# Three moves in a two-layer gated cross-attention kernel: context moments taken early, wider layer-norm chains, and expert products in split fp32r

## Chip, cores and metric

One core of one Trainium2 chip. The metric is the device time of one execution in microseconds (us), launch to end. The core has five engines with a queue each: TensorE (PE, with its weight loads shown apart as PEld), VectorE (DVE), ScalarE (ACT), GpSimd (POOL) and SyncE (SP, which here only issues transfers). They run side by side and meet at semaphores; each engine takes its own instructions strictly in the order in which the program lists them.

## What is computed

Two layers over x (4 batches of 256 tokens, 128 features) and a context (4 batches of 512 tokens, 128 features):

```python
x = x + tanh(g_xattn[0]) * L0_xattn(layernorm(x), ctx)       # 16 heads of 8, q and k normalised per head
x = x + tanh(g_ffn[0])   * L0_ffn(layernorm(x))              # shared gated FFN, top-2 of 8 LoRA experts
x = x + tanh(g_xattn[1]) * L1_xattn(ctx, layernorm(x))       # 16 heads of 64
x = x + tanh(g_ffn[1])   * L1_ffn(layernorm(x))              # top-1 of 8 full experts

def L1_xattn(c, latents):            # queries from latents, keys and values from both
    c, lat = layer_norm(c, ln_m_g, ln_m_b), layer_norm(latents, ln_l_g, ln_l_b)
    kv_in = concat(c, lat)
    ...
def L1_ffn(x):
    idx = argmax(softmax(x @ gate_w + gate_b, axis=1), axis=-1)
    for e in range(8):
        h = gelu(x @ W1[e] + b1[e])                          # 128 -> 512
        out += where(idx == e, h @ W2[e] + b2[e], 0)         # 512 -> 128
```

A layer norm is (t - mean) * rsqrt(var + 1e-5) over the 128 features. The context's mean and variance depend on the input `ctx` alone, the tokens' on the running x.

## The kernel before

Everything stays in on-chip memory; a token tile is 128 tokens, so a batch has TQ = 2 token tiles and TC = 4 context tiles. The order of work is written out by hand for every engine, one function per step of an engine, and steps of different engines meet at one semaphore per kind of step.

**First attention** (about 47 to 190 us). `AQ` = 16 turns of four heads each. In turn q PE makes score maxima of turn q+2 (`row_max0`, eight products into two banks in turn), scores of turn q (`scores0`), values of turn q-1; ACT the exponentials; POOL four multiplies per turn that mask the queries (`masked0`, L513); DVE eight maxima (L1047) and one `divide0` (L1054, L1058). A product of `row_max0` may write its bank only when DVE has read the product two before it.

**First FFN** (190 to 300 us). One pass per batch: DVE runs `hidden0`, `route0`, `norm_b`, `down0`, `lora0`, `residual_b`. After batch 0 DVE also takes the moments and the reciprocal root of context batch 0 and normalises it (`context_stats(0)`, `context_scale(0, 0)`, `context_scale(0, 1)`, `context_norm(0)`), after batch 1 the same for the tokens of batch 0.

**Second attention** (300 to 711 us). `G1` = 32 pairs of heads; g = 8 b + p is pair p of batch b. Per pair DVE has three row maxima (`row_max1`, L1291 and L1294, and the small L1300 `max_cols`), two low halves of the projections of pair g+3 (`proj_low`, L1282 `kql`), and a division (`divide1`, L1307 `RECIPROCAL` and L1308). Two slots per pair, `first_slot(g)` (before the third maximum) and `second_slot(g)` (after it), hold the preparation of the next batch: for b < 3 the moments (p = 0), the reciprocal root by halves (p = 1, 2) and the normalising (p = 3), of context in the first slot and of tokens in the second. For b = 3 they hold the norms of token batches 0 and 1 for the last stage, and its first routing. Each reciprocal root is a chain of dependent instructions on 128x4 or 128x2 values: L1216 or L1232 first, then L1201, L1202 and three (first half) or six (second half) of L1205, L1206, L1207. PE issues the products of all this in a fixed order; in pair p = 1 of batches 1 to 3 it also makes the output projection of the batch before (`outputs1`, 32 fp32 instructions into bank 7, which the half 1 of `project(g+3)` used just before: it waits until `proj_low(g+3, 1)` has read it). POOL sums the exponentials (L540, L543, L548).

**Second FFN** (711 us to the end). Per batch i: PE `hidden1(i, 0..3)`, each 8 fp32 products of 128x128 weights and 256 masked token columns (`xm`) and one bias product; ACT the gelu and a rounded copy `hid1_h`; POOL the low part `hid1_l` in two halves (L556); PE `down1(i, 0)`, `down1(i, 1)` in split fp32r. A split product is three fp32r products, high by high, high by low, low by high. In between PE, ACT and DVE route batch i+1: `turned_in1`, `head1`, `route1`, softmax, `probs1`, `masks1`, `wide_masks1`, `masked` (DVE writes `xm` in two halves, L1394), `bias1`. An fp32 product appears in the trace as two matmul instructions, an fp32r product as one.

## Time and profile before

| | us |
|---|---|
| median of 3 runs (850.34 to 851.39) | 851.11 |
| the profiled execution | 852.44 |
| its span, first to last instruction | 850.4 |

The profiled execution is thus 1.33 us over the median, and 2.04 us of it lie around the span.

```profile
PE 748.1 (88%) x5558; PEld 550.1 (65%) x5558; DVE 587.3 (69%) x1169; ACT 357.6 (42%) x528; POOL 287.9 (34%) x207
PEclk9789999997999999999998999899999999999999
PE 64%; DVE 24%; issue 7%; ACT 3%; DMA 1%; POOL 0%; SPq 0%; POOLq 0%; DVEq 0%; ACTq 0%
```

The first line is busy time, share of the span and instructions of each engine. The second cuts the span into 40 slices and gives the TensorE clock granted in each, in tenths of full speed, 2.4 GHz. The third is the chain of work that ended last, by engine. Matmul ends are modelled, and matmuls overlap: the rate of a run of matmuls is read from the distance of their starts, not from their durations.

### The profile page before, as it was taken

How to read it: one execution, taken by the hardware profiler on the slowest of the kernel's cores; microseconds unless marked ns; L12 is line 12 of the kernel's file. 1: busy time of each engine (PE TensorE's matmuls, PEld its weight loads, DVE VectorE, ACT ScalarE, POOL GpSimd, SP SyncE). 2: the span in 40 equal slices, each digit the busy share in tenths (PEclk: the TensorE clock that was granted, in tenths of full speed). 3: DMA queues.
4: the chain of work that ended last, by engine and by line, in shares of the span. 5: the costliest groups of instructions: out<-in, count | busy, mean ns of one | idle time of the engine just before them, and what ended most of it. 6: DMA issues, size and time to landing. Idle time of an engine off the chain costs nothing.

```text
span 850.4 us, 14161 instructions
## 1 busy us (share of the span) xinstructions
PE 748.1 (88%) x5558; PEld 550.1 (65%) x5558; DVE 587.3 (69%) x1169; ACT 357.6 (42%) x528; POOL 287.9 (34%) x207
## 2 busy tenths in 40 slices
PE   6779999977888978899979998889989878989896
PEld 5656666646777755667656675656756556867784
DVE  4767676727887777886878769787788784446243
ACT  2567676653342454355524553245534443130200
POOL 4364443300111023455533455245543462010100
PEclk9789999997999999999998999899999999999999
DMA  9000000013000030000000000000000000000000
GB/s 173 6 1 2 1 3 1 2 67 132 1 1 1 0 99 1 2 1 2 1 1 2 1 2 1 1 2 1 2 1 2 1 1 1 1 7 2 6 7 6
DMA packets 25553, 11.55 MB, mean 14 GB/s; under 512 B 11832, under 2 KB 24200, under 8 KB 25360
## 3 DMA queue, kind: packets, MB, share of 16 engines
q1 hardware_dynamic: 24480, 10.59, 4.9%
q8 instruction: 44, 0.72, 0.3%
q10 hardware_dynamic: 1008, 0.07, 0.1%
q14 instruction: 21, 0.17, 0.1%
HBM read 10.06 MB, written 0.52 MB: 12 GB/s over the span
## 4 chain that ended last, share of the span: by engine, by line
PE 64%; DVE 24%; issue 7%; ACT 3%; DMA 1%; POOL 0%; SPq 0%; POOLq 0%; DVEq 0%; ACTq 0%
PE ps L1536 61%; DVE pmax L1294 2%; DVE kql L1282 2%; DVE o L1307 2%; PE ps L1547 2%; DVE rt_t L1206 1%; DVE pmax L1291 1%; DVE max_cols L1300 1%; ACT v L562 1%; ACT kqh L562 1%; DVE ysum L1413 1%; DVE cn L948 1%; DVE rs_t L924 1%; DVE rt_t L1205 1%; DVE xnC L1239 1%
## 5 line engine op out<-in xcount | busy, mean ns | idle before, releaser
L803 ACT ACTIVATE p<-ps 128x1024 f32<-128x1024 f32 x96 | 96.4, 1025 | 147.1 <-PE ps L1536 144.7
L1536 PE MATMUL ps<-p,v 128*64 128x256 f32 (+1 forms) x1280 | 131.4, 388 | 5.1 <-DVE o L1308 2.3
L540 POOL TENSOR_TENSOR acc<-p 128x1024 f32<-128x1024 f32 x32 | 76.7, 2397 | 168.7 <-ACT p L803 168.7
L1536 PE MATMUL ps<-kqh 64*128 64x256 f32 (+1 forms) x640 | 106.6, 371 | 12.5 <-DVE pmax L1291 4.7
L1047 DVE TENSOR_REDUCE mx<-ps 128x1 bf16<-128x512 f32 x128 | 82.5, 687 | 36.3 <-PE ps L1536 36.0
L1291 DVE TENSOR_REDUCE pmax<-ps 128x2 f32<-128x1024 f32 x64 | 78.2, 1222 | 39.2 <-PE ps L1536 38.3
L543 POOL TENSOR_TENSOR acc<-acc,p 128x1024 f32<-128x1024 f32 x32 | 76.2, 2380 | 70.7 <-ACT p L803 70.7
L1536 PEld LDWEIGHTS ps<-p,v 128*64 128x64 f32 (+1 forms) x1280 | 63.7, 126 | 54.9 <-issue 19.3
L1536 PEld LDWEIGHTS ps<-kqh 64*128 64x128 f32 x640 | 59.0, 195 | 38.3 <-issue 28.7
L513 POOL TENSOR_SCALAR q<-qst,rmask 128x256 fp32r<-128x256 f32 x64 | 58.7, 936 | 59.0 <-ACT qst L562 59.0
L658 ACT ACTIVATE p<-ps 128x1024 f32<-128x1024 f32 x64 | 65.4, 1025 | 22.3 <-PE ps L1536 20.4
L1282 DVE TENSOR_TENSOR kql<-ps,kqh 128x512 fp32r<-128x512 f32 x64 | 44.1, 690 | 26.9 <-ACT kqh L562 26.4
L1536 PE MATMUL ps<-xm,w 128*128 128x256 f32 x256 | 58.7, 381 | 2.7 <-DVE xm L1394 2.7
L1307 DVE RECIPROCAL o<-ps 128x256 f32<-128x256 f32 x32 | 56.1, 1752 | 5.9 <-PE ps L1536 4.3
L1536 PE MATMUL ps<-max_row,onesb 64*128 64x256 bf16 x384 | 57.2, 284 | 0.0
L1536 PE MATMUL ps<-kqh,kql 64*128 64x256 f32 x384 | 56.9, 283 | 0.0
L1536 PE MATMUL ps<-kql,kqh 64*128 64x256 f32 x384 | 56.3, 279 | 0.0
L1536 PEld LDWEIGHTS ps<-xm,w 128*128 128x128 f32 x256 | 47.4, 190 | 10.7 <-DVE xm L1394 3.5
L556 POOL TENSOR_TENSOR hid_l<-hid,hid_h 128x512 fp32r<-128x512 f32 x8 | 10.1, 1264 | 115.2 <-ACT hid_h L562 115.2
L1536 PE MATMUL ps<-kst,q 128*128 128x512 f32 x128 | 47.2, 427 | 0.8 <-DVE mx L1047 0.5
L1536 PE MATMUL ps<-q,kst 128*128 128x256 f32 x256 | 46.7, 304 | 0.4 <-ACT p L658 0.4
L1294 DVE TENSOR_REDUCE pmax<-ps 128x4 f32<-128x1024 f32 x32 | 39.1, 1222 | 10.1 <-PE ps L1536 9.7
(268 smaller groups left out, 1526.2 us busy)
## 6 DMA issues: line engine op xcount, KB each, us to landing
w<-in_L_ffn_W_dram SPq DMA_DIRECT2D x1, 2048.0 KB, 12.6
wt<-in_L_ffn_W_dram SPq DMA_DIRECT2D x4, 512.0 KB, 6.1
ctx_all<-in_ctx_dram SPq DMA_DIRECT2D x4, 256.0 KB, 5.2
raw_kv<-in_L_xattn_Wkv_dram SPq DMA_DIRECT2D x1, 1024.0 KB, 5.1
raw<-in_L_ffn_B_dram SPq DMA_DIRECT2D x9, 64.0 KB
xr<-in_x_dram SPq DMA_DIRECT2D x4, 128.0 KB, 3.8
raw_q<-in_L_xattn_Wq_dram SPq DMA_DIRECT2D x1, 512.0 KB, 6.1
wout<-in_L_xattn_Wout_dram SPq DMA_DIRECT2D x1, 512.0 KB, 7.4
```

What stands on the lines that cost most here:

```text
L513: pool.tensor_scalar(q4[:, q % SLOTS, v, :], qst[:, q % 2, :], rmask[:, v:v + 1], None, ALU.mult).then_inc(g_q4.sem, 1)
L540: pool.tensor_tensor(acc1[:, :], p1[:, s, 0, :], p1[:, s, 1, :], ALU.add).then_inc(g_acc.sem, 1)
L543: pool.tensor_tensor(acc1[:, :], acc1[:, :], p1[:, s, 2, :], ALU.add).then_inc(g_acc.sem, 1)
L562: return act.activation(to, of, ACT.Copy)
L658: act.activation(p0[:, n % PR0, :], bank(2 * (n % 2), 2), ACT.Exp).then_inc(a_exp0.sem, 1)
L803: act.activation(p1[:, g % 2, u, :], bank(2 * (n % 2), 2), ACT.Exp, scale=SCALE1).then_inc(a_exp1.sem, 1)
L1047: dve.tensor_reduce(mx0[:, q % 2, n % 2, n // 2:n // 2 + 1], bank(4 + m % 2), AX, ALU.max).then_inc(d_max0.sem, 1)
L1282: dve.tensor_tensor(kql[:, g % KS, at], bank(X_BANK.get(("proj", g, half), 7)), kqh[:, g % KS, at], ALU.subtract).then_inc(d_kql.sem, 1)
L1291: dve.tensor_reduce(pmax[:, g % 2, 0, part, :], m.rearrange("p (j k) -> p j k", j=2), AX, ALU.max).then_inc(d_max1.sem, 1)
L1294: dve.tensor_reduce(pmax[:, g % 2, 1, :, :].rearrange("p t j -> p j t"), m.rearrange("p (j t k) -> p j t k", j=2, t=TQ), AX, ALU.max).then ...
L1307: then(dve.reciprocal(o1[:, g % OS, :], bank(6)[:, NQ:2 * NQ]))
L1536: return pe.matmul(o, lhsT, rhs, start=start, stop=stop)
```

## The change

1. **Context moments.** A new `spare_slot(q)` at the end of each turn of the first attention on DVE: q = 2 to 5 take the moments of context batch q-2, q = 6 and 7 the two halves of the reciprocal root of all 16 tiles at once. The calls in the first FFN and in the slots of the second attention go; only `context_norm` stays.
2. **Shared token chains.** The tokens of batches 1 to 3 have their moments taken in pair 0 and their reciprocal root in pair 1 of the second attention, together. The norms of batches 0 to 2 for the last stage have theirs in pairs 2 and 3 of batch 3 and are applied in pair 4 (0 and 1) and later (2). Several small steps of the last pairs move too.
3. **Expert input products** of batches 1 to 3 become split fp32r: ACT rounds `w1` to `w1_h` in four parts, DVE makes `w1_l`, ACT and DVE split the tokens, DVE writes masked high and low tokens instead of one `xm`. The steps of PE, ACT and DVE in the last stage are put in another order, and the second half of `hid1_l` goes from POOL to DVE.

Left out of the diff below: new buffers and semaphores, and functions that only get new index arguments.

```diff
+            def spare_slot(q):
+                if 2 <= q < 2 + B:
+                    context_stats(q - 2)
+                if q - 2 - B in (0, 1):
+                    context_scale(q - 2 - B)
...
                 if q >= 1:
                     divide0(q - 1)
+                spare_slot(q)
...
                 if i == 0:
-                    context_stats(0)
-                    context_scale(0, 0)
-                    context_scale(0, 1)
                     context_norm(0)
...
             def first_slot(g):
+                if b + 1 < B and p == 3:
+                    context_norm(b + 1)
+                if g == 0:
+                    dve.wait_ge(d_xB.sem, B)
+                    dve.wait_ge(d_xnC.sem, 1)
+                    tokens_stats(range(TQ, 2 * TQ), 0)
+                if g == 1:
+                    tokens_scale(rest, 0, True)
+                if b == B - 1:
+                    if p == 2:
+                        tokens_stats(range(0, 2 * TQ), 0)
                     if p == 3:
+                        tokens_scale(rest, 0, False)
                     if p == 4:
+                        tokens_norm(xnD[:, 0, :, :], x_of(0), 0).then_inc(d_xnD.sem, 1)
+                    if p == 6:
+                        masks1(0)
+            def second_slot(g):
+                if b + 1 < B and p == 3:
+                    latents_norm(b + 1)
+                if g == 0:
+                    tokens_stats(range(2 * TQ, B * TQ), TQ)
+                if g == 1:
+                    tokens_scale(rest, 1, True)
+                if b == B - 1:
+                    if p == 2:
+                        tokens_stats(range(2 * TQ, 3 * TQ), 2 * TQ)
+                    if p == 3:
+                        tokens_scale(rest, 1, False)
+                    if p == 4:
+                        tokens_norm(xnD[:, 1, :, :], x_of(1), TQ).then_inc(d_xnD.sem, 1)
                         step(dve.memset(probT[:, :], 0.0))
                     if p == 5:
                         route1(0)
...
                 second_slot(g)
                 if g + 3 < G1:
                     proj_low(g + 3, 1)
+                if g == G1 - 1:
+                    masked(0, 0)
                 if g >= 1:
                     divide1(g - 1)
                 if g == G1 - 3:
                     probs1(0)
+                    w2_low(0)
                 if g == G1 - 2:
+                    w2_low(1)
                     wide_masks1(0)
                 if g == G1 - 1:
-                    masked(0, 0)
-                    w2_low(FC - 1)
                     masked(0, 1)
+                    w2_low(2)
+                    w2_low(3)
             divide1(G1 - 1)
             for i in range(B):
                 if i + 1 < B:
                     route1(i + 1)
+                    tokens_low(i + 1)
                     probs1(i + 1)
+                if i == 0:
+                    for c in range(E // 2):
+                        w1_low(c)
+                if i + 1 < B:
                     masks1(i + 1)
                     wide_masks1(i + 1)
+                hidden_low(i)
                 if i == 0:
                     residual_c(B - 1)
+                if i + 2 < B:
+                    norm_d(i + 2)
+                if i + 1 < B:
+                    masked(i + 1, 0)
                 select1(i, 0, 0)
                 select1(i, 0, 1)
                 if i + 1 < B:
-                    masked(i + 1, 0)
+                    masked(i + 1, 1)
                 summed1(i, 0)
-                if i + 2 < B:
-                    norm_d(i + 2)
                 select1(i, 1, 0)
                 select1(i, 1, 1)
-                if i + 1 < B:
-                    masked(i + 1, 1)
                 summed1(i, 1)
                 residual_d(i)
...
             bias_out(0)
+            w1_high(0)
             for i in range(B):
                 if i + 1 < B:
                     routed(i + 1)
+                    act.wait_ge(a_xTD.sem, i + 2)
+                    copy(xT_h[:, (i + 1) % 2, :], xTD[:, (i + 1) % 2, :]).then_inc(a_xTh.sem, 1)
+                    if i == 0:
+                        for c in range(1, E // 2):
+                            w1_high(c)
+                    softmax(i + 1)
                 for n in range(2):
...
                 for e in range(E):
                     if c == 0 and e % 4 == 0:
                         pe.wait_ge(d_xm.sem, 2 * i + e // 4 + 1)
+                    if i == 0:
+                        mm(o, w1[:, e, c * P:(c + 1) * P], xm[:, e, :], e == 0, False)
+                        continue
+                    if i == 1 and c == 0 and e % 2 == 0:
+                        pe.wait_ge(d_w1L.sem, e // 2 + 1)
+                    mm(o, w1_h[:, e, at], xm_h[:, e, :], e == 0, False)
+                    mm(o, w1_h[:, e, at], xm_l[:, e, :], False, False)
+                    mm(o, w1_l[:, e, at], xm_h[:, e, :], False, False)
...
+                if g == G1:
+                    wide_masks1(0, 1)
+                    bias1(0)
                 if g >= 1:
                     values1(g - 1, (0, 1, 2, 3))
...
             for i in range(B):
                 ahead = i + 1 < B
+                if ahead:
+                    turned_in1(i + 1)
                 hidden1(i, 0)
                 if ahead:
-                    turned_in1(i + 1)
+                    head1(i + 1)
                 hidden1(i, 1)
                 if ahead:
-                    head1(i + 1)
+                    probs1(i + 1)
                 hidden1(i, 2)
-                if ahead:
-                    probs1(i + 1)
                 hidden1(i, 3)
                 if ahead:
                     masks1(i + 1)
                 if i == 0:
                     outputs1(B - 1)
-                down1(i, 0)
                 if ahead:
                     wide_masks1(i + 1, 0)
-                down1(i, 1)
+                down1(i, 0)
                 if ahead:
                     wide_masks1(i + 1, 1)
                     bias1(i + 1)
+                down1(i, 1)
```

## Rows read from the trace of the kernel before

**Rows 1.** Engine busy time by stretch: us, busy (instructions) of PE, PEld, DVE, ACT, POOL; PEclk, DMA
```profile
414.00:462.00 48.00, 41.17 (x337) 29.48 (x336) 37.94 (x56) 16.86 (x24) 20.23 (x11) 0.89 0.00 1
618.00:664.00 46.00, 38.56 (x342) 27.21 (x342) 38.62 (x56) 16.80 (x24) 20.55 (x11) 0.96 0.00 1
744.00:779.40 35.40, 31.58 (x152) 25.47 (x149) 16.55 (x48) 6.66 (x11) 2.52 (x2) 0.95 0.02 4
767.00:770.40 3.40, 3.40 (x10) 2.65 (x9) 0.39 (x1) 0.00 (x0) 0.00 (x0) 0.52 0.00 0
```

**Rows 2.** DVE in order of time (start, us, instruction [idle before]): one reciprocal per pair
```profile
413.87 1.76 DVE L1307 RECIPROCAL o<-ps 128x256 f32<-128x256 f32 x1
427.89 1.75 DVE L1307 RECIPROCAL o<-ps 128x256 f32<-128x256 f32 x1
446.53 1.75 DVE L1307 RECIPROCAL o<-ps 128x256 f32<-128x256 f32 x1
504.95 1.76 DVE L1307 RECIPROCAL o<-ps 128x256 f32<-128x256 f32 x1
515.91 1.76 DVE L1307 RECIPROCAL o<-ps 128x256 f32<-128x256 f32 x1
```

**Rows 3.** PE in order of time, second attention and last stage: idle before and its releaser
```profile
428.03 5.47 PE L1536 MATMUL ps<-wout,o 128*128 128x128 f32 x32 [2.76 <-DVE kql L1282]
728.49 3.74 PE L1536 MATMUL ps<-wout,o 128*128 128x128 f32 x32
```

**Rows 4.** DVE and POOL at one instruction of the chain on 128x2 values
```profile
344.01 2.26 DVE L1206 TENSOR_TENSOR rt_t<-rt_t,rt_v 128x2 f32<-128x2 f32 x1
343.88 2.37 POOL L543 TENSOR_TENSOR acc<-acc,p 128x1024 f32<-128x1024 f32 x1 [5.79 <-ACT p L803]
```

**Rows 5.** DVE, then PE, in the first FFN
```profile
228.80 0.86 DVE L939 BATCH_NORM_STATS2 stats<-ctx_all 128x6 f32<-128x128 f32 x4
230.12 0.17 DVE L1216 TENSOR_SCALAR rs_v<-moments 128x4 f32<-128x4 f32 x1
232.51 1.11 DVE L948 TENSOR_SCALAR cn<-ctx_all,moments,rs_y 128x128 f32<-128x128 f32 x4
234.96 3.69 PE L1536 MATMUL ps<-um,wt 128*128 128x256 f32 x16 [2.00 <-DVE hid L1159]
```

**Rows 6.** First attention, one turn: DVE twice, PE, POOL
```profile
83.81 1.28 DVE L1047 TENSOR_REDUCE mx<-ps 128x1 bf16<-128x512 f32 x2
91.58 1.28 DVE L1047 TENSOR_REDUCE mx<-ps 128x1 bf16<-128x512 f32 x2
85.28 0.64 PE L1536 MATMUL ps<-kst,q 128*128 128x512 f32 x2
84.54 3.62 POOL L513 TENSOR_SCALAR q<-qst,rmask 128x256 fp32r<-128x256 f32 x4 [4.14 <-ACT qst L562]
```

**Rows 7.** PE: two fp32r products of 256 columns; an fp32 group; two waits
```profile
422.33 0.28 PE L1536 MATMUL ps<-kv_h,wq_h 128*128 128x256 f32 x1
422.45 0.28 PE L1536 MATMUL ps<-kv_l,wq_h 128*128 128x256 f32 x1
715.67 3.62 PE L1536 MATMUL ps<-xm,w 128*128 128x256 f32 x16
719.13 0.59 PE L1536 MATMUL ps<-wt,b 128*128 128x256 f32 x2
747.75 1.99 PE L1536 MATMUL ps<-xm,w 128*128 128x256 f32 x8 [1.35 <-DVE xm L1394]
765.68 0.50 PE L1536 MATMUL ps<-w_h,hid_h 128*128 128x512 f32 x1 [2.47 <-POOL hid_l L556]
```

**Rows 8.** A group of instructions: busy us, mean ns | idle before
```profile
L1394 DVE TENSOR_TENSOR xm<-ps,xTD 128x1024 f32<-128x1024 f32 x8 | 9.7, 1218 | 0.3 <-PE ps L1536 0.3
```

**Rows 9.** PE and DVE at the seam into the last stage
```profile
707.14 1.95 PE L1536 MATMUL ps<-p,v 128*64 128x256 f32 x16 [2.32 <-DVE o L1308]
711.56 3.62 PE L1536 MATMUL ps<-xm,w 128*128 128x256 f32 x16
```

202 lines of the change are left out of this document (118 added, 84 removed).

## The prediction

> **What bounds the kernel now.** I read the chain of waits first: 64% of it is PE and 24% DVE, so PE sets the time except where DVE holds it up. The table of busy time by stretch says where. In the first 48 us of batch 1 of the second attention PE is busy 41.2 us and its clock stands at 0.89 of full speed; in batch 3 it is busy 38.6 of 46 us at 0.96 [rows 1]. DVE is busy 38 us in both, and its order of time gives the pair times: 10.96 us for a pair with empty slots, against 14.02 and 18.64 us for pairs that contain the preparation of the next batch, and 102.04 us for the eight [rows 2]. PE's order of time shows how DVE gets into its way: it waited 2.76 us for the low half of a projection, which stood in DVE's queue behind the reciprocal roots, and the 32 instructions of the output projection after it took 5.47 us, against 3.74 us in the last stage [rows 3]. A wait costs twice: after it the granted clock is at 0.52 for 3.4 us, the lower of the two levels, 1.2 GHz, in the one case of which I show the stretch [rows 1]. In the last stage a batch takes 35.4 us [rows 1] and contains two waits, 1.35 us for `xm` and 2.47 us for `hid_l` [rows 7]. The first attention shows PE without a gap that has a releaser.
>
> **First attention: a cost.** A spare slot puts a chain between `divide0` and the next two maxima. The same steps stand in the first FFN: from the first statistic to the first scale step 1.32 us, from there to the first normalising 2.39 us for twelve steps, so 1.3 us for a moments slot and 1.2 us for a scale slot, which has six [rows 5]. In a turn the two maxima start at 83.81 and are 1.28 us of work; PE's third and fourth maxima products start at 85.28 and may write only when these are read [rows 6]. Started 1.3 us later, the two end at about 86.4, and the fourth product, which would start at about 85.5, waits 0.9 us more. That is not made up, as everything behind it on PE (values, scores) waits in order: 4 x 0.95 + 2 x 0.85 = 5.5 us. The scale slots also meet POOL's four multiplies of 3.62 us, which begin 0.7 us into the slot [rows 6]. How these two get along is read from the second attention: a step on 128x2 values took 2.26 us, ending with the POOL instruction that had begun 0.13 us before it [rows 4], against 0.17 us for a free one [rows 5]. One POOL multiply is 0.9 us; I add 0.6 for each scale slot. Taken: **+6.7**; from +1 (DVE's idle time in a turn takes most of it) to +12 (both scale slots held to the end of all four multiplies, 3 us each).
>
> The Trainium skill (SBUF — State Buffer, Who interferes with whom) says that a DVE instruction with two SBUF inputs and a GpSimd instruction that reads SBUF exclude each other for a whole instruction, and that one with at most one input outside the fast modes does not contend. The trace agrees for the 2.26 us step, which has two inputs. By the rule the four moments slots would stay unstretched and only the scale slots pay, which is what the sum above assumes for another reason, the time at which POOL starts.
>
> **First FFN: a gain.** The 3.7 us between 228.80 and 232.51 go [rows 5]. PE's 2.00 us wait for `hid` at 234.96 ends with them; then PE's own products are last, so no more than the wait is gained: **-2.0** (from -1 to -3).
>
> **Second attention: the main gain.** Eight clean pairs and one output projection at 3.74 us are 91.4 us, against 102.04 [rows 2, 3]: 10.6 us, the lost clock included. In batches 1 and 2 all chains leave pairs 0 to 2; the two norms in pair 3 remain and may hold a projection's low half as before, so I take -10.0 each; batch 2 repeats the pattern of batch 1. In batch 0 pairs 0 and 1 keep as many instructions as they had (six tiles instead of four and two, twelve scale steps of another width); only pair 2 becomes empty: -2.5 (0 to -5). In batch 3 PE is idle 7.4 us of 46, and loses 1.8 by the clock [rows 1]. Two chains become one, later: moments in pair 2, twelve steps in pair 3, four normalising instructions in pair 4. Pairs 0 and 1 are freed, pairs 3 and 4 loaded; also two of four `w2_low` steps, 1.2 us each by the width of [rows 8], move behind the division. I take -5.5 of 9.2. Together **-28.0** (from -15, if half the chains' delay returns at the norms and in pairs 3 and 4, to -33). New here: `first_slot(0)` waits for `d_xB`, which DVE itself has signalled before, and nothing queues behind that.
>
> **The seam: a cost.** PE's `turned_in1(1)` now stands ahead of `hidden1(0, 0)` and waits for the last division. Before, PE waited 2.32 us at 707.14 and began the products at 711.56 [rows 9]. `wide_masks1(0, 1)` and `bias1(0)`, 1 us, now fill that wait, so the last sums end near 710.5. The division after them is 2.2 us (1.76 [rows 2] and its multiplication of about 0.4), and all of `hidden1(0)` waits behind the transposes: they begin near 712.85, where before the products began at 711.56. **+1.3** (0 to +3, as a wait of 2.4 us may bring 3.4 us at half clock).
>
> **Last stage: a gain.** A group of eight fp32 products takes 3.46 us from its first instruction to the bias product [rows 7]. Split, it is 24 fp32r products; two such, 256 columns wide and with a weight load each, start 0.12 us apart [rows 7]: 2.88 us, and I add 0.1 for the change of kind. Four groups: -1.9 per batch. Twelve groups of 0.48 are 5.8 us. The 1.35 us wait for `xm` goes, because `wide_masks1(i+1, 0)` now stands ahead of `down1(i, 0)` and DVE writes the first masked half during it. That costs DVE two instructions of 1.22 us per half instead of one [rows 8], for which it has room: it is busy 16.6 us of 35.4 [rows 1]. What queues behind the second masked half on DVE is the first sum of experts, 2.2 us, for which PE does not wait. The 2.47 us wait for `hid_l` shrinks by 0.7 (512 columns on DVE, half of an instruction of [rows 8], instead of 1.3 us on POOL) and by the 0.4 us of `wide_masks1` that now lies in it. With a wait of about 1.5 us left I expect no stretch at half clock: 3.4 us at 0.52 gave away 1.7 [rows 1]. Batches 1 and 2: -(1.9 + 1.35 + 0.7 + 0.4 + 1.7) = -6.1 each; batch 3, which routes no further batch and had its `xm` early, keeps only the groups and the faster low half: -2.6. In batch 0 nothing of this, but four `w1_low` (4.9 us by the width of [rows 8]) precede `masks1(1)` on DVE; they end some 2 us before PE asks for the masks, and their ACT copies lie beside the fp32 products. If `w1_low` ran later, PE would wait before `masks1(1)`. ACT now does softmax(i+1) ahead of gelu(i, 0), and so waits for DVE's `route1`: the group of products behind it is 3.4 us, the chain about 3.1 us, so gelu is just in time. Together **-14.8** (from -8, if the stretches at half clock remain and gelu comes late, to -17).
>
> **The sum.** +6.7 - 2.0 - 28.0 + 1.3 - 14.8 = -36.8 us. From the profiled execution, 852.44 (span 850.4): 815.6 us. The median was 1.33 us lower: 851.11 - 36.8 = **814.3 us**.
>
> **The rivals.**
> - *The delay returns later in the second attention* (0.18). The norms of pair 3 and the loaded pairs 3 and 4 of batch 3 hold the low half as the chains did, with the clock stretches after it. For it: a norm is as exposed to POOL as a scale step. Against: pair 2 to 3 cost little. With -15 for -28: 827.3 us.
> - *Everything fits* (0.20). The first attention costs 1 (DVE's idle time takes it), the second gives 33, the last stage 17, the seam 0: 851.11 + 1 - 2 - 33 - 17 = 800.1 us.
> - *The split products are not faster* (0.04): each of 24 takes the 0.216 us of one of the 16 instructions in [rows 7], so 5.2 us per group where I took 2.98. That is 12 x 2.2 = +26.6: 840.9 us. The 0.12 us of a like pair speaks against it.
> - *Slower* (0.04): the spare slots. Gains without them are 43.5 us, so they decide from 7.25 us for each of six. A turn is 7.77 us [rows 6]; if a slot made PE's maxima miss a whole turn, because DVE and POOL hold each other and the masked queries for the next turns come late, six turns are 46.6 us: 851.11 + 46.6 - 43.5 = 854.2 us. Against it: moments ran beside POOL unstretched, and queries are masked turns ahead.
> - Within 0.2% (0.02): costs of that rival between 41.8 and 45.2 us.
>
> **Chances and range.** 0.2%, 1.7 us, is about what a measurement of this kernel can tell from no change. My forecast, 808 to 821, has 0.52. Range 802 to 829: it takes in the first rival and most of the bounds above, and leaves out most of the second and the others. Faster 0.94, same 0.02, slower 0.04.
>
> **What would show it.** Right: turns 2 to 7 of the first attention longer by 0.9 to 1.4 us; no wait at the `hid` of the first FFN; batches 1 and 2 at 91 to 93 us; a PE wait near 2.4 us ahead of the first transposes of the last stage; groups of 24 products in about 2.9 us; batches 1 and 2 of the last stage near 29 us. Wrong: turns 2 to 7 unchanged or over 2 us longer; half-clock stretches in pairs 1 to 3 of batches 1 and 2; PE waiting for `w1_l` or for `masks1`.

## The result, and the profile after

The changed kernel takes 825.94 us (median of 4 runs, 825.83 to 827.83), the kernel before beside it 850.73 (849.72 to 851.39): ratio 0.9715, 95% interval 0.9697 to 0.9732. Forecast were 814.3 us and a range of 802 to 829. The direction and the range held; of the 36.8 us forecast, 24.8 came. The profiled execution took 827.83 us with a span of 826.0.

The page of the changed kernel: busy time, and the chain that ended last by engine.

```profile
PE 740.4 (90%) x5654; PEld 549.9 (67%) x5654; DVE 574.0 (69%) x1100; ACT 360.6 (44%) x533; POOL 282.4 (34%) x203
PE 71%; DVE 20%; issue 4%; ACT 3%; DMA 1%; SPq 0%; DVEq 0%; ACTq 0%
```

PE has 71% of the chain where it had 64%, DVE 20% where it had 24%. By stretch, with the same columns as [rows 1]:

```profile
418.00:466.00 48.00, 45.43 (x414) 32.61 (x415) 35.31 (x39) 20.96 (x30) 24.11 (x12) 0.96 0.01 1
619.00:665.00 46.00, 41.10 (x379) 28.75 (x377) 34.04 (x59) 19.08 (x26) 20.09 (x11) 0.96 0.01 1
763.00:792.40 29.40, 27.67 (x186) 24.27 (x185) 18.24 (x33) 6.97 (x12) 1.29 (x1) 1.00 0.02 5
323.00:330.00 7.00, 6.34 (x42) 4.45 (x40) 2.52 (x9) 2.43 (x4) 0.78 (x1) 0.51 0.01 2
```

In the first 48 us of batch 1 PE is now busy 45.4 us instead of 41.2. In batch 3 DVE is less busy than before (34.0 of 46 us instead of 38.6), and PE gained only 2.5 us. The third row is batch 2 of the last stage and the first half microsecond of batch 3: from first product to first product batch 1 takes 29.4 us and batch 2 28.9 us, instead of 35.4 and 35.3. The last row is new: 7 us at half clock at the start of the second attention. The reciprocals, as in [rows 2] (divisions 7, 8, 9 and 15, counted from 0), then the output projection:

```profile
419.83 1.76 DVE L1359 RECIPROCAL o<-ps 128x256 f32<-128x256 f32 x1
430.30 1.76 DVE L1359 RECIPROCAL o<-ps 128x256 f32<-128x256 f32 x1
443.92 1.76 DVE L1359 RECIPROCAL o<-ps 128x256 f32<-128x256 f32 x1
513.23 1.76 DVE L1359 RECIPROCAL o<-ps 128x256 f32<-128x256 f32 x1
431.05 3.73 PE L1627 MATMUL ps<-wout,o 128*128 128x128 f32 x32
```

Batch 1, from division 7 to 15, takes 93.40 us instead of 102.04; the pair that took 18.64 us takes 13.62, and the output projection 3.73 us with no wait ahead of it, where [rows 3] had 2.76 + 5.47.

All stages stand in one table, worked out from the start times of DVE's reciprocals in the profiled execution of each kernel. "1st att." is from the first division of the first attention to its last, "FFN" from there to division 1 of the second attention (first FFN and start of the second attention), then divisions 1 to 8, 8 to 16, 16 to 24, 24 to 31, and from 31 to the end. Totals of one kernel lay up to 9 us apart, with a lower mean granted clock in the longer runs, and the FFN column differs by up to 4 us between kernels that are the same there, so a move of 1 to 3 us is read from its own column.

```
                 1st att.    FFN    b.0     b.1     b.2     b.3     last    span
before            111.39  160.05  80.78  102.20  104.81   76.23   139.27   850.4
changed           118.04  157.59  78.93   93.40   93.40   81.05   127.85   826.0
x1_fill           118.22  158.65  78.98   92.72   92.71   82.67   127.91   825.6
x2_norms          118.26  153.46  78.33   92.11   92.06   83.05   127.96   817.4
x3_spread         112.06  157.15  78.93   93.37   93.40   81.01   127.86   819.8
x4_onemax         118.26  152.54  78.92   92.67   92.64   84.19   129.57   820.8
x5_seam           118.30  157.66  78.93   93.39   93.41   81.08   124.51   820.8
x6_batch3         118.27  157.31  78.94   93.39   93.40   79.47   129.35   825.7
x7_all            112.05  154.07  78.32   92.09   92.07   79.33   124.97   808.8
x8_split_only     111.29  159.96  80.76  102.20  104.75   79.92   128.62   841.2
x9_late_slot      112.04  146.71  76.50   90.22   91.02   75.66   124.93   790.2
x10_fill_start    118.04  156.73  78.93   92.65   92.69   84.32   129.62   826.5
x11_best          112.03  146.06  76.46   90.22   91.03   74.03   120.61   782.5
x12_w2_back       118.24  157.37  78.94   93.39   93.39   80.51   127.86   825.2
```

The first two lines show where the 24.4 us of span went: first attention +6.65, FFN -2.46, batches 0 to 2 of the second attention -1.85, -8.80 and -11.41, batch 3 **+4.82**, last stage -11.42.

Two things limit what totals can tell. The stretch ahead of the first division, in which the kernels are the same but for one tile of moments, isn't in the table and takes 72.0 to 76.0 us. And the time at half clock is spread differently in every kernel. What it gives away, time times (1 - PEclk), is in the columns of the table from FFN to last: 10.2, 0, 5.1, 5.1, 0 and 4.1 us in the kernel before, and 13.7, 0, 1.7, 1.7, **6.8** and 2.3 in the changed one. Batch 3, the column that became longer, is the one where half clock came in.

### The profile page after: what moved, and what is told of

Its sections match the earlier page's. It is cut to its first block, busy times and chain, and to the rows that moved or that the text cites. A ratio compares the mean times of both kernels' runs of the same rounds, so it can differ in the third digit from the quotient of the medians.

```text
span 826.0 us, 14271 instructions
## 1 busy us (share of the span) xinstructions
PE 740.4 (90%) x5654; PEld 549.9 (67%) x5654; DVE 574.0 (69%) x1100; ACT 360.6 (44%) x533; POOL 282.4 (34%) x203
## 4 chain that ended last, share of the span: by engine, by line
PE 71%; DVE 20%; issue 4%; ACT 3%; DMA 1%; SPq 0%; DVEq 0%; ACTq 0%
PE ps L1627 68%; PE ps L1638 2%; DVE mx L1068 2%; DVE o L1359 2%; ACT v L572 1%; DVE max_cols L1352 1%; DVE pmax L1343 1%; DVE pmax L1346 1%; DVE xnC L1285 1%; DVE kql L1334 1%; DVE ysum L1494 1%; DVE cn L1296 1%; ACT kqh L572 1%; PE ps L1731 1%; DMA raw<-in_L_xattn_Wproj_dram 1%
## 5 line engine op out<-in xcount | busy, mean ns | idle before, releaser
L1627 PE MATMUL ps<-kqh 64*128 64x256 f32 (+1 forms) x640 | 109.9, 379 | 11.9 <-ACT v L572 4.3
L1627 PEld LDWEIGHTS ps<-kqh 64*128 64x128 f32 x640 | 62.0, 202 | 37.6 <-issue 29.5
L1627 PE MATMUL ps<-max_row,onesb 64*128 64x256 bf16 x384 | 59.8, 293 | 0.0
L1627 PE MATMUL ps<-kqh,kql 64*128 64x256 f32 x384 | 59.5, 292 | 0.0
L1627 PE MATMUL ps<-kql,kqh 64*128 64x256 f32 x384 | 58.8, 288 | 0.0
L1627 PE MATMUL ps<-kst,q 128*128 128x512 f32 x128 | 49.1, 435 | 4.6 <-DVE mx L1068 4.2
L1627 PEld LDWEIGHTS ps<-q,kst 128*128 128x128 f32 x256 | 34.5, 189 | 13.5 <-issue 7.0
L572 ACT ACTIVATE kqh<-ps 128x512 fp32r<-128x512 f32 x64 | 38.0, 594 | 11.0 <-PE ps L1627 8.5
L1627 PEld LDWEIGHTS ps<-kqh,kql 64*128 64x128 f32 x384 | 41.9, 201 | 0.5
```

The costliest lines, as they stand in the source:

```text
L572: return act.activation(to, of, ACT.Copy)
L1627: return pe.matmul(o, lhsT, rhs, start=start, stop=stop)
```

## The experiments

My theory when the experiments began: the missing 12 us are half-clock stretches that I had taken to go with the waits. The rival: DVE's small steps hold PE elsewhere than before.

**The clock.** Products into a bank that nobody reads fill three kinds of waits: at the start of the second attention, in pair 3 of batches 0 to 2 (shown below), and ahead of the first down product of the last batch.

```diff
+                            pe.wait_ge(a_mrow.sem, g + 2)
+                            filler(bank(4)[:, NQ:2 * NQ], kqh[:, s, 0:P], kqh[:, s, NK:NK + NQ], 16)
                             context_turn(use[1])
...
```

> The changed kernel with products that nobody reads, put on TensorE into waits that are there anyway: 18 before the first maxima row of the second attention (the wait of 2.67 us at 322.51), 16 before the transposes of cn in pair 3 of batches 0, 1 and 2 (waits of 2.29, 2.30 and 2.30 us), 16 before the first down product of the last batch (2.12 us). Nothing is computed differently. Theory 'clock': the half-clock stretches behind these waits come from TensorE standing still in them. Then those at 323 to 330 (3.3 us lost), 459.5 to 463 and 551.5 to 555 (1.75 each) and 807.5 to 811 (1.75) vanish, 8.5 us: about 817.5 us. Rival 'the stretches come whatever TensorE does in a wait of 2 us': as many stretches as before and 826 us, or some tenths more where the added products run over.

Measured: 827.13 us (824.88 to 829.93), ratio to the kernel before 0.9677 (0.9619 to 0.9736). In pair 3 the products do what they should, here in batch 1, first the changed kernel, then this one:

```profile
458.09 0.66 PE L1638 MATMUL ps<-ident,cn 128*128 128x128 f32 x4 [2.30 <-DVE kql L1334]
```
```profile
457.42 0.66 PE L1642 MATMUL ps<-ident,cn 128*128 128x128 f32 x4 [0.43 <-DVE kql L1334]
```

The stretches behind them are gone, but batches 1 and 2 are only 0.7 us shorter each, where the granted clock had given away 1.7. And x4_onemax, which leaves these three waits of 2.3 us as they are, has no stretch behind any of them and the same 92.7 us. The third fill is worth more: the last batch, whose stretch at 807.8 is gone, takes 32.5 us instead of 34.1. The total doesn't show it, because a stretch now lies at 700.5 and makes the first batch of the last stage 1.7 us longer, and because batch 3 of the second attention, where nothing was changed, is 1.6 us longer. The 18 products at the start stood ahead of the wrong row, where TensorE didn't wait, so that fill was tried again.

```diff
+                    if g == 0:
+                        filler(bank(6)[:, 0:NQ], kqh[:, 0, 0:P], kqh[:, 0, NK:NK + NQ], 20)
                     if g + 1 < G1:
                         max_row_in(g + 1)
```

> The changed kernel with 20 products that nobody reads, on TensorE in the wait of 2.67 us at 322.51 that ends at the second maxima row of the second attention (in the earlier trial they stood ahead of the first row, which is not where TensorE waits). Theory 'the two stretches at half clock that follow, 323 to 330, come from standing still in that wait': they go, and up to 3.4 us with them: 822.5 us. Rival 'they come by the time at which the wait falls, or from what stands before it': one or both stay, 826 us.

Measured: 828.30 us (823.85 to 831.01), ratio 0.9720 (0.9683 to 0.9757). The wait in the changed kernel, then in this one, here with the stretch of 7 us behind it:

```profile
322.51 0.28 PE L1627 MATMUL ps<-negidentb,max_cols 128*128 128x128 bf16 x2 [2.67 <-DVE max_cols L1352]
```
```profile
320.27 0.28 PE L1627 MATMUL ps<-negidentb,max_cols 128*128 128x128 bf16 x2 [0.32 <-DVE max_cols L1352]
320.30:327.30 7.00, 6.13 (x55) 4.15 (x57) 4.21 (x13) 4.15 (x6) 1.91 (x2) 1.00 0.01 2
```

The clock there is 1.00 instead of 0.51, as the clock theory says. From the last instruction that writes `zm` (the end of the first FFN) to division 0 2.4 us are gained of the 3.4, but the next pair is 1.6 us longer, so up to division 1 it is 0.9 us.

In the places that were filled the stretches explain 3.9 us of the missing 12 (0.7 and 0.7, 1.6 in the last batch, 0.9 at the start). **But no fill reached batch 3**, and there the record shows half clock at work. From division 27 to 31, the kernel before and the changed one:

```profile
674.00:711.13 37.13, 29.50 (x306) 19.47 (x305) 29.07 (x41) 15.72 (x21) 22.70 (x11) 1.00 0.01 2
657.66:698.15 40.49, 33.81 (x309) 23.02 (x307) 29.97 (x42) 16.55 (x23) 20.38 (x11) 0.87 0.01 1
```

It takes 3.4 us longer for nearly as many matmuls, and PE isn't idle longer in it (6.7 us, before 7.6) but busy longer: 10 us of it run at half clock (671.3 to 674.7 and 681.5 to 688.3), which gives away 5.1 us, and in the kernel before none. What a stretch costs at this place two later kernels tell, whose programs are the same here, x9_late_slot and x11_best, from division 28 to 29:

```profile
636.62:649.35 12.73, 9.91 (x90) 6.38 (x88) 9.68 (x22) 4.82 (x7) 6.12 (x4) 0.87 0.01 1
634.87:645.97 11.10, 8.27 (x90) 5.70 (x88) 9.60 (x22) 4.82 (x7) 6.12 (x4) 1.00 0.01 1
```

One stretch more, and 1.63 us more, nearly the 1.7 it gives away. So a stretch costs 0.7 us in one place and 1.6 in another, and the clock theory, which the totals seem to refute, holds for a good part of the 12 us when it is read by stages.

**What the waits hang on.** The last step of the maxima, with one read instead of two:

```diff
-  dve.tensor_tensor(max_cols[..], pmax[:, g % 2, 0, :, :], pmax[:, g % 2, 1, :, :], ALU.max)
+  dve.tensor_reduce(max_cols[..], pmax[:, g % 2, :, :, :].rearrange("p a t j -> p t j a"), AX, ALU.max)
```

> The changed kernel with the last step of the maxima, max_cols, as a maximum over one read of pmax (tensor_reduce) instead of one of two reads (tensor_tensor). It takes 0.18 us alone and 2.0 to 2.1 us when GpSimd's sum of 1024 columns runs; TensorE waits for it four times (2.67, 1.22, 1.24 and 2.13 us). Theory 'an instruction with two reads of SBUF is held until GpSimd's instruction ends, one with a single read is not': max_cols is 0.2 us everywhere, 1.0 to 1.9 us of each of the four waits go, about 6 us in sum, and up to 8 more by the half-clock stretches at 323, 340, 650 and 681 behind them: 812 to 820 us. Rival 'any small instruction of VectorE is held': it stays at 2 us where GpSimd runs, and 826 us.

Measured: 827.51 us (822.67 to 831.95), ratio 0.9698 (0.9625 to 0.9771). The instruction, min/median/max in ns, in the changed kernel and in this one:

```profile
L1352 DVE TENSOR_TENSOR max_cols<-pmax x32: 175/177/2082, 312.0 to 679.4; 128x4 bf16<-128x4 f32 x32
```
```profile
L1352 DVE TENSOR_REDUCE max_cols<-pmax x32: 172/173/177, 306.3 to 669.1; 128x4 bf16<-128x8 f32 x32
```

So the mechanism is shown: the form with two reads is held by GpSimd, the form with one is not. The total is not the 812 to 820 us of the theory. The FFN column is 5 us shorter (1.9 of wait and 3.4 of clock expected), but 2.2 of them lie in the first FFN, where nothing was changed and a half-clock stretch is missing; behind `zm` it is 2.9 us. PE waits for `pmax` instead, 3.04 us at 334.1 and 2.98 us at 638.8, where the changed kernel has 1.24 for `max_cols` and 1.84 for `pmax`: the steps behind `max_cols` are now the ones that are held. In batch 3 the gain was lost again and more, 84.19 us instead of 81.05. DVE, POOL and PE there:

```profile
672.42 2.32 DVE L1547 TENSOR_TENSOR w_l<-wt,w_h 128x1024 fp32r<-128x1024 f32 x1
674.66 2.95 DVE L1434 TENSOR_SCALAR maskb<-iota_ed,topf 128x1024 bf16<-128x1024 bf16 x2
672.38 1.28 POOL L559 TENSOR_TENSOR fold<-acc 128x512 f32<-128x512 f32 x1
674.25 2.69 POOL L551 TENSOR_TENSOR acc<-p 128x1024 f32<-128x1024 f32 x1 [0.59 <-ACT p L813]
677.67 1.03 PE L1627 MATMUL ps<-identb,maskb 128*128 128x128 bf16 x8 [4.20 <-DVE maskb L1434]
```

The wait of 2.13 us for `max_cols` is gone. The low half of w2 now falls under the fold (2.32 us instead of 1.21), the masks behind it under the next sum (2.95 instead of 0.87), and PE waits 4.20 us. Kernels x1, x2 and x10 have the same wait of 4.2 us and a batch 3 of 82.7 to 84.3 us, although their instructions there are those of the changed kernel: a small shift in time is enough to fall from one pattern into the other.

**The norms of pair 3.**

```diff
-                if b + 1 < B and p == 3:
+                if b + 1 < B and p == 2:
                     context_norm(b + 1)
...
-                if b + 1 < B and p == 3:
-                    latents_norm(b + 1)
...
                     proj_low(g + 3, 1)
+                if b + 1 < B and p == 3:
+                    latents_norm(b + 1)
```

> The changed kernel with the context norm of the next batch in pair 2 instead of pair 3 and the token norm of pair 3 behind the low half of the projection instead of ahead of it. Theory 'the norms hold the low half': TensorE's three waits of 2.3 us for kql before the transposes of cn go, and with them the stretches at half clock at 459.5 and 551.5 (1.75 us each): 6.9 + 3.5 = 10.4 us, 815.5 us. If the stretches only move to another wait: 6.9 us, 819 us. Rival 'the queue of VectorE is as long as before and what stands behind the norm is late instead' (the division of the pair before, which the next values wait for): 824 to 826 us, with a wait for o in place of that for kql.

Measured: 819.23 us (819.16 to 828.10), ratio 0.9618 (0.9539 to 0.9698). The total looks like the first theory. But of the 8.6 us of span 3.6 lie ahead of the first division and 4.1 in the FFN column, where nothing was changed: other half-clock stretches. The three waits for `kql` are gone, and the batches are shorter by 0.6, 1.3 and 1.3 us, not by 2.3 and more; PE waits for `pmax` instead. The rival names the kind of loss, though not its place.

**The spare slots.** One tile at each of two places in a turn (k = 0 ahead of the last two maxima, k = 1 at the end) instead of four in one slot:

```diff
-                if 2 <= q < 2 + B:
-                    context_stats(q - 2)
+                n = 2 * (q - 1) + k
+                if 0 <= n <= B * TC:
+                    context_tile(n)
```

> The changed kernel with the spare slots of the first attention cut up: one context tile (one bn_stats, and the bn_aggr of the tile before) at each of two places in turns 1 to 9 and two steps of the reciprocal root at each of two places in turns 9 to 12, instead of four tiles in one slot of turns 2 to 5 and six steps in one of turns 6 and 7, which cost 1.05 to 1.22 us a turn. Theory 'a turn has about 0.3 us of slack for VectorE in front of its maxima' (1.35 us of slot cost 1.05): two pieces of about 0.45 us cost 0.1 each or nothing, some 20 pieces at most 2 us, so 4.5 to 6.5 us come back: 819.5 to 821.5 us. Rival 'every step of VectorE in these turns is paid in full': 826 us or some more, since the pieces have waits of their own.

Measured: 820.55 us (816.16 to 822.13), ratio 0.9584 (0.9523 to 0.9645). First attention 112.06 us instead of 118.04: 6.0 of the 6.65 us come back, and the theory stands. Turns with moments are as long as in the kernel before (7.76 us); only the three with the steps of the root cost 0.2 each.

**The seam.** In batch 0 the head and the probabilities move one group down as well.

```diff
-                if ahead:
+                if ahead and i >= 1:
                     turned_in1(i + 1)
                 hidden1(i, 0)
+                if i == 0:
+                    turned_in1(i + 1)
...
```

> The changed kernel with the order of TensorE in the first batch of the last stage as in the kernel before: a group of products ahead of the transposes for batch 1, of the head, and of the probabilities. Theory 'the 2.41 us wait for the last division is paid in full': the products begin 2.4 us earlier and the chain of masks for batch 1 has as many products in front of it as before: 823.5 us. Rival 'the masks come late instead' (the copies and low halves of w1 now stand ahead of them on VectorE, 4.9 us): TensorE waits at the transposes of the masks and at most 0.5 us is gained.

Measured: 822.63 us (819.95 to 824.55), ratio 0.9660 (0.9630 to 0.9690). The products begin with no wait ahead of them,

```profile
696.17 3.72 PE L1627 MATMUL ps<-xm,w 128*128 128x256 f32 x16
```

the masks are waited for 0.4 us, and the last stage is 3.3 us shorter. Of this 1.6 us are the stretch at 807.5, which this run doesn't have (the last batch takes 32.5 us instead of 34.1). From the last division to the first product of batch 1 it is 1.7 us, so of the wait of 2.4 us not all comes back.

**Batch 3.**

```diff
-                    if p == 2:
-                        tokens_stats(range(0, 2 * TQ), 0)
+                    if p == 0:
+                        tokens_stats(range(0, TQ), 0)
...
-                    w2_low(1)
                     wide_masks1(0)
                 if g == G1 - 1:
                     masked(0, 1)
+                    w2_low(1)
...
+                    scores1(g, 1)
                     if g == G1 - 2:
                         probs1(0)
-                    scores1(g, 1)
```

> The changed kernel with three moves in batch 3 of the second attention. The moments of tiles 0 to 3 in pair 0 instead of pair 2; the low half of w2's second quarter behind the wide masks instead of ahead; TensorE's transposes of the probabilities after the second group of scores instead of after the first. Theory 'the batch is longer than I forecast because small steps stand in the wrong pair': pair 2 to 3 is 1.3 us shorter (14.89 to about 13.6), the wait of 1.25 us for probT goes, and the half-clock stretch behind it if it hangs on that wait: 2.5 to 4.2 us, 821.7 to 823.4 us. Rival 'the pairs are held by max_cols, which GpSimd holds, whatever else is moved': the waits of 1.24 and 2.13 us stay and the sum of the pairs of batch 3 changes by under 1 us: 825.5 us.

Measured: 822.68 us (819.51 to 827.56), ratio 0.9651 (0.9615 to 0.9687). By stages the theory falls: batch 3 is 1.6 us shorter, the last stage 1.5 us longer. Pair 3 (divisions 25 to 26) takes 14.88 us as in the changed kernel, so the moments of pair 2 cost nothing there. What is left is the twelve steps in pair 3 itself, which x9_late_slot will show.

**The five together.**

> The changed kernel with the spread slots, the norms moved, the one-read max_cols, the moves in batch 3 and the old order of the first batch of the last stage together. If the parts add: 6.0 us in the first attention (measured), 0.6 us in each of three batches and 0.7 us of clock in two by the norms (measured), 1.9 us of wait and up to 3.4 us of clock at the start of the second attention, 5 us in batch 3, where max_cols no longer hands its delay to the wide masks (81.05 us for seven pairs before, 76 us or less expected), 2.4 us at the seam: about 22 us less than the changed kernel, 804 us. If the waits of batch 3 only change places: 809 us. If the seam's gain is lost at the masks too: 811 us.

Measured: 807.02 us (805.57 to 810.68), ratio 0.9474 (0.9451 to 0.9496). They add nearly, except in batch 3, which stays at 79.33 us where under 76 was expected. The steps of the root there, and PE behind them:

```profile
628.21 2.03 DVE L1273 TENSOR_TENSOR rt_t<-rt_y 128x6 f32<-128x6 f32 x1
630.47 1.13 DVE L1275 SCALAR_TENSOR_TENSOR rt_y<-rt_t,rt_y 128x6 f32<-128x6 f32 x1
627.84 2.37 POOL L554 TENSOR_TENSOR acc<-acc,p 128x1024 f32<-128x1024 f32 x1 [2.04 <-ACT p L813]
630.29 1.29 POOL L559 TENSOR_TENSOR fold<-acc 128x512 f32<-128x512 f32 x1
636.23 0.49 PE L1641 MATMUL ps<-kqh 64*128 64x512 f32 x2 [2.98 <-DVE pmax L1355]
```

The second slot begins right behind `max_cols`, and there POOL's second sum and its fold run, 3.65 us of every pair. That gave the next kernel.

```diff
-                second_slot(g)
+                if g == G1 - 3:
+                    second_slot(g)
                 if g + 3 < G1:
                     proj_low(g + 3, 1)
-                if b + 1 < B and p == 3:
-                    latents_norm(b + 1)
...
                 if g >= 1:
                     divide1(g - 1)
+                if g != G1 - 3:
+                    second_slot(g)
+                if b + 1 < B and p == 3:
+                    latents_norm(b + 1)
```

> The kernel with all five earlier moves, with one more: the second slot of every pair of the second attention (moments, halves of the reciprocal root, token norms) stands behind the division of the pair before, not ahead of it, except the one that routes. In the run before this one the small steps of that slot began right behind max_cols and fell under GpSimd's sum: in pair 3 of batch 1 the two norm instructions took 2.76 us instead of 0.6 and TensorE then waited 1.71 us for pmax; in pair 3 of batch 3 two of the six steps took 2.03 and 1.13 us instead of 0.17, and TensorE waited 2.98 us. Theory 'what is late is the next maximum, by what GpSimd holds': behind the division GpSimd is done, so 1.7 us come back in each of batches 0 to 2 and about 2.6 us in batch 3: 7.7 us less, 799 us. Rival 'VectorE has no room in these pairs wherever the slot stands': the wait stays, and 806 to 808 us.

Measured: 794.54 us (789.09 to 797.01), ratio 0.9329 (0.9287 to 0.9370). Against x7_all the FFN column is 7.4 us shorter, the batches 1.8, 1.9, 1.05 and 3.7 us. Of the FFN column 2.5 us lie in the first FFN, where nothing was changed and two half-clock stretches are missing; from `zm` on it is 4.9 us, the steps of pairs 0 and 1 and one stretch less. Another 2.8 us of span lie ahead of the first division, also unchanged. So the move itself is worth 13.3 of the 18.6 us between the two profiled executions. Pair 3 of batch 3, where the twelve steps stand, takes 11.28 us instead of 14.71. The two norm instructions of pair 3 in the changed kernel, and here:

```profile
453.69 3.74 DVE L1285 TENSOR_SCALAR xnC<-xr,token_moments,rt_y 128x128 f32<-128x128 f32 x2
```
```profile
435.07 0.69 DVE L1297 TENSOR_SCALAR xnC<-xr,token_moments,rt_y 128x128 f32<-128x128 f32 x2
```

Nothing was taken from DVE: the same steps stand behind the division, where POOL is at its end (in pair 3 of batch 3 3.4 us behind the start of `max_cols`, in x7_all 0.1). **This is what the prediction lacked.**

**One part alone.** Parts one and two undone, the split products kept.

> The changed kernel with its first two parts undone: moments and reciprocal roots of context and tokens in the slots of the second attention where the kernel before has them, nothing in the first attention; the split products and the order of the last stage stay. Theory 'the parts are separate': first attention 6.6 us shorter than in the changed kernel, batches 1 and 2 back at 102 and 104 us, last stage as in the changed kernel, 851.1 - 11.4 = 839.7 us. Of batch 3, where the changed kernel is 4.1 us slower than the kernel before in pairs 5 and 6: if the steps that the third part moved there (halves of w2, probabilities) are the cause, it stays slow: 843.8 us; if the longer chain of the second part is, it is as before: 839.7 us.

Measured: 843.36 us (843.04 to 843.74), ratio 0.9908 (0.9889 to 0.9926). The parts are separate: first attention, FFN and batches 0 to 2 agree with the kernel before to 0.1 us. But of batch 3 the divisions 27 to 31 take 40.8 us and not 37.1 as before. Here the loss comes with the third part alone, which moved steps there: a low half and the masks behind it fall under POOL's fold and sum, and PE waits 4.20 us for the masks.

```profile
695.23 2.32 DVE L1549 TENSOR_TENSOR w_l<-wt,w_h 128x1024 fp32r<-128x1024 f32 x1
697.48 2.95 DVE L1438 TENSOR_SCALAR maskb<-iota_ed,topf 128x1024 bf16<-128x1024 bf16 x2
```

The changed kernel takes nearly the same, 40.5 us, but not for this reason. It has no such wait, its masks take 0.48 us each and its low halves of w2 1.21 to 1.22 us, undisturbed:

```profile
683.50 1.21 DVE L1547 TENSOR_TENSOR w_l<-wt,w_h 128x1024 fp32r<-128x1024 f32 x1
```

What it has instead are three times as many microseconds at half clock (10.2 for 3.4). The two equal sums are made of different things.

**The low halves of w2.**

```diff
+                if g >= G1 - FC + 1:
+                    w2_low(g - (G1 - FC + 1))
...
                     probs1(0)
-                    w2_low(0)
                 if g == G1 - 2:
-                    w2_low(1)
                     wide_masks1(0)
                 if g == G1 - 1:
+                    w2_low(3)
                     masked(0, 1)
-                    w2_low(2)
-                    w2_low(3)
```

> The changed kernel with the four low halves of w2 on VectorE where the kernel before has them: the first three in the second slots of the last three pairs, ahead of the division, the fourth between the two masked halves. What is known: from the fourth to the last division of batch 3 the kernel before takes 37.1 us, the changed kernel 40.5, and the kernel with its first two parts undone 40.8 with a wait of 4.2 us for maskb, so these 3.4 to 3.7 us belong to the third part. Theory 'the low half of w2 ahead of the wide masks': it goes, the seven pairs of batch 3 take 77.5 us instead of 81.05, and the whole 822.5 us. Rival 'only the place changes': in the run with one of the four moved behind the masks batch 3 was 1.6 us shorter and the last stage 1.5 us longer, because the last division came later; then the sum of batch 3 and last stage stays at 208.9 us, and the whole at 826 us.

Measured: 823.27 us (819.54 to 827.03), ratio 0.9651 (0.9611 to 0.9692). Batch 3 80.51 us, last stage 127.86, in sum 0.5 us less: the rival. Back in their old place they now take

```profile
667.62 3.14 DVE L1549 TENSOR_TENSOR w_l<-wt,w_h 128x1024 fp32r<-128x1024 f32 x1
681.42 1.22 DVE L1549 TENSOR_TENSOR w_l<-wt,w_h 128x1024 fp32r<-128x1024 f32 x1
686.50 3.38 DVE L1549 TENSOR_TENSOR w_l<-wt,w_h 128x1024 fp32r<-128x1024 f32 x1
693.91 2.30 DVE L1549 TENSOR_TENSOR w_l<-wt,w_h 128x1024 fp32r<-128x1024 f32 x1
```

where the kernel before had 1.21 to 1.22 us for each, and the changed kernel too. In these runs no single place is good or bad; the meeting with POOL's sums costs, and that shifts with everything ahead of it.

**The last stage, and the best version.** On top of x9_late_slot:

```diff
-                pe.wait_ge(d_hidL.sem, i + 1)
...
                     for c in range(FC):
+                        if t == n == 0 and c == 2:
+                            pe.wait_ge(d_hidL.sem, i + 1)
```

> The kernel with the late slots and one more change in the last stage: the down products of a batch begin with the two quarters of hid whose low halves GpSimd has written long before; TensorE waits for VectorE's half, which is ready 1.46 us after it asks, only ahead of the third quarter. Six split products of 0.23 us, 1.4 us, stand in front of that wait. If they cover it: 1.4 us in each of four batches, 5.6 us less than the kernel with the late slots: about 793.5 us. If TensorE then waits as long at the next place (the wide masks behind the first down products, or the select of the batch before): 798 us.

Measured: 791.85 us (784.35 to 793.27) beside 850.58 us of the kernel before: ratio 0.9289 (0.9255 to 0.9323). The last stage is 4.3 us shorter than in x9_late_slot, not 5.6. Of this about 1.6 us are a half-clock stretch less in the last batch (so much as in x1_fill and x5_seam), so the change gives 2.7 us: 1.4 in each of batches 2 and 3 and nothing in 0 and 1. PE waits once 0.7 us for the half and once, in batch 1, 1.64 for `xm_l`, the place that the expectation named for a loss. This version is faster than both kernels; against x9_late_slot the medians are 2.7 us apart and the ranges overlap. The profiled execution is the fastest of six. Its clock from 260 to 779 us:

```profile
260.00:779.00 519.00, 492.90 (x4150) 373.20 (x4149) 366.80 (x566) 215.83 (x314) 203.15 (x102) 1.00 0.02 6
```

PE is busy 95% there, waits at most 1.8 us, and no stretch at half clock is left in these 519 us. Summed over windows of 0.5 us of the whole span, the time times (1 - PEclk) is 34.6 us in the changed kernel, 32.9 in the kernel before and 15.0 here.

## Why the prediction was right, and where not

- **First attention, +6.7: right** in size, and the reason nearly. 6.65 us; turns 2 to 7 are longer by 1.04, 1.05, 1.06, 1.04, 1.22 and 1.07 (0.9 to 1.4 stood in the prediction). The 0.6 us added to each scale slot for the meeting with POOL didn't come: the held steps took 0.41 and 0.26 us instead of 0.17. Four moments slots that cost 0.1 us more than forecast each, and 0.2 us in turn 12, make up for it. That the sum came out to 0.05 us is luck. DVE's slot, and PE's late maxima in the turn behind it:

```profile
92.69 0.86 DVE L1112 BATCH_NORM_STATS2 stats<-ctx_all 128x6 f32<-128x128 f32 x4
94.00 2.64 DVE L1068 TENSOR_REDUCE mx<-ps 128x1 bf16<-128x512 f32 x4
94.84 1.01 PE L1627 MATMUL ps<-kst,q 128*128 128x512 f32 x2 [0.52 <-DVE mx L1068]
```

  The slot is 1.31 us (92.69 to 94.00) and unstretched, against rows of the first FFN [rows 5]. The slack in front of the maxima, about 0.3 us, was read rightly from [rows 6], and x3_spread is the same fact used the other way. That PE has no gap with a releaser holds for the turns that I read, not for the stage: it waits 4.5 us there in all, in the kernel before.
- **First FFN, -2.0: right.** 1.9 us from the first transposes of `xnB` to those of `cn`; PE's wait of 2.00 us for `hid` [rows 5] is gone; its waits for the product's result were 4.6 us in two and are 2.6 in one.
- **Batches 1 and 2, -10.0 each: right in sum.** From division 7 to 15 and from 15 to 23, -8.64 and -10.75. Of the difference to the forecast in batch 1, 0.7 us are clock (x1_fill) and 0.6 the norms (x2_norms).
- **Start and batch 0, -2.5: wrong.** The first reciprocal comes 3.0 us later after `zm` than before, the pairs behind it gain 1.85, in sum +1.1. The step that failed: "pairs 0 and 1 keep as many instructions as they had". As many, but `max_cols` is held (2.67 us of wait, as before), the steps behind it too, and 7 us at half clock followed, which the kernel before did not have there. Without the first of the two stretches (x10_fill_start) the first reciprocal comes only 0.6 us late. With the slots late (x9_late_slot) the time from `zm` to division 1 falls by 4.9 us against x7_all and batch 0 by 1.8.
- **Batch 3, -5.5: wrong, and the largest miss.** From division 23 to 31 it is +0.45, so 6 us. The gain itself came: the two pairs that lost their chains (divisions 23 to 25) are 5.8 us shorter. The step that failed is what the rest was priced at. I had seen that [rows 4] a step on small values took 2.26 us instead of 0.17 when POOL's sum ran, and priced such a meeting for the first attention; for the moved chain in pair 3 I used undisturbed steps of 0.2 us. Two of the twelve are held, 1.13 us under a sum and this one, 1.25, under the fold, and PE waits 1.84 us behind it (1.04 in the kernel before):

```profile
642.90 1.25 DVE L1262 TENSOR_TENSOR rt_t<-rt_t,rt_v 128x6 f32<-128x6 f32 x1
648.98 0.49 PE L1627 MATMUL ps<-kqh 64*128 64x512 f32 x2 [1.84 <-DVE pmax L1343]
```

  Pair 3 takes 14.88 us instead of 13.57, +1.3. The second thing is half clock, which I had put at nothing here: behind this wait comes a stretch (650.8 to 654.2), and the pair with it takes 12.06 us instead of 10.45. In x1_fill, with the same instructions, the stretch lies earlier and the pair takes 10.46: +1.6. Then divisions 27 to 31, 40.5 us instead of 37.1, with 10 us at half clock. The moved halves of w2, priced at 1.2 us, took 1.21 to 1.22, so they were priced rightly. Of PE's waits there only the one for `probT` grew, by 0.8 us (1.25), and this one is as long as in the kernel before (2.13 us at 695.69):

```profile
681.52 0.39 PE L1627 MATMUL ps<-negidentb,max_cols 128*128 128x128 bf16 x2 [2.13 <-DVE max_cols L1352]
```

  In the changed kernel half clock follows it, in the kernel before it doesn't. Why stays open, and no run removed the half clock in these pairs alone, so how much of the 3.4 us it makes is read from the traces and not tested.
- **The seam, +1.3: right in kind.** The wait ahead of the transposes is 2.41 us, as forecast; from the last division to the first products it is 2.61 us, before 0.43, so +2.2.
- **Last stage, -14.8: batches 1 and 2 right**, 6.0 and 6.5 us for 6.1 each. Here the start and end of a group of 24 products, and the wait for the low half:

```profile
733.60 0.36 PE L1627 MATMUL ps<-xm_h,w_h 128*128 128x256 f32 x1
736.55 0.59 PE L1627 MATMUL ps<-wt,b 128*128 128x256 f32 x2
750.43 0.47 PE L1627 MATMUL ps<-w_h,hid_h 128*128 128x512 f32 x1 [1.46 <-issue]
807.50:811.50 4.00, 4.00 (x11) 3.10 (x11) 0.00 (x0) 0.00 (x0) 0.00 (x0) 0.57 0.00 0
```

  2.95 us for 2.98 forecast; a wait of 1.46 us for 1.5 and no half clock behind it, where [rows 7] had 2.47. In batch 3 the wait is 2.12 us and half clock follows (the last row), so 1.1 us came of 2.6; with that wait filled (x1_fill) the batch is 1.6 us shorter.
- **The price of a stretch.** I took 1.7 us for each that goes. In pair 3 of batches 1 and 2 a stretch is worth 0.7 us, and at the start two are worth 0.9 up to division 1; in the last pairs of batch 3 and in the last batch one is worth 1.6. I had also taken them to go with the waits: the changed kernel gives away 34.6 us and the kernel before 32.9. My reading of the difference is that DVE and ACT set the pace in parts of the cheap ones; no run isolates it.
- **The rivals.** "The delay returns later in the second attention" gave 827.3 us and named pairs 3 and 4 of batch 3 as its place. 825.9 was measured, nearer to it than to my 814.3. I gave it 0.18; [rows 4] would have carried more. Pairs 3 and 4 are 2.9 of the 6 us, so it has about half of the miss in this batch. Its other half, the norms in pair 3, cost only 0.6 us a batch. "Split products not faster" and "slower by the spare slots" are excluded by the rows above, and "everything fits" by batch 3.

## What to carry to other kernels

Price a moved step by where it lands beside the other engines, not by its shortest duration: here a step of 0.17 us that met GpSimd's sum took as long as the rest of the sum, up to 2 us. In a pipeline with a fixed period, find the part of the period in which the other engine works (here 3.65 us behind the third exponential) and put the small steps elsewhere; moving them behind the division was worth 12.5 us in the median (807.0 to 794.5), and 13.3 us by the columns that it touches, half of what the change itself gave. And a wait that is removed is worth at most the time until the next one: 2.3 us of wait were worth 0.6. Last, compare the clock stage by stage before a theory of the clock is dropped: a stretch of 3.4 us at half clock cost from 0.7 to 1.6 us by its place, and one that is removed can come back elsewhere.

## What the runs showed of the hardware

- **Held instructions.** `max_cols` with two reads: 175 to 2082 ns; with one read, 172 to 177 ns, with POOL's sums beside it in both kernels. The Trainium skill (SBUF — State Buffer, Who interferes with whom) says that an instruction with two SBUF inputs is kept out by a GpSimd instruction that reads SBUF, and that `tensor_reduce` never contends; both agree. It also says that the port pair which the two share is an exclusive lock. That agrees too, in both directions: in x12_w2_back the low half that began at 681.42 took its 1.22 us, and POOL's sum, 0.17 us behind it, 3.30 us instead of 2.37:

```profile
681.59 3.30 POOL L554 TENSOR_TENSOR acc<-acc,p 128x1024 f32<-128x1024 f32 x1 [1.97 <-ACT p L813]
```

- **Not beside every GpSimd instruction.** In the first attention of the changed kernel a step with two reads ran its 0.17 us while POOL multiplied, and the next one took 0.26:

```profile
130.47 0.17 DVE L1105 TENSOR_TENSOR rc_t<-rc_t,rc_v 128x16 f32<-128x16 f32 x1
130.39 0.96 POOL L524 TENSOR_SCALAR q<-qst,rmask 128x256 fp32r<-128x256 f32 x1 [5.36 <-ACT qst L572]
```

  The multiply reads SBUF, so by the rule it should have held the step to 131.35; the measurement decides. Starts and ends on POOL are rough in a profile, and no run was made of it.
- **Chains are held step by step.** A chain of six steps of 0.17 us met the sum with its first step (2.03 us) and the fold with its third (1.13 us): 4.0 us instead of 1.2.
- **Half clock behind a wait is not certain.** The same three waits of 2.3 us for `kql` were followed by stretches in batches 1 and 2 but not in batch 0 of the changed kernel, x3, x5, x6 and x12, and in none of the three in x4 and x10. The instructions around these waits are the same in all of them; what differs is the time at which they fall. When the waits go, the stretches behind them go (pair 3 of batches 1 and 2 in x2_norms and x9_late_slot). The Trainium skill (TensorE: Matmul & The Clock Gate, Part 1: The HAM clock gate) says that the state depends on how busy PE has been recently; the runs agree with that. No run here tells which of two equal waits is followed by a stretch.
